# The first norm of a fused LSTM, attention and expert kernel: normalised tokens made on POOL instead of DVE

## The reference, cut to what matters

```python
x = _L0_conv_ref(x, ...)                  # 16 recurrent steps over the rows of the image
t = _to_tokens(x)                         # 16 images x 256 tokens x 96 channels
t = t + _L1_attn_ref(_ln_t(t), ...)       # 6 heads, 256 tokens read as causal windows below
t = t + _L1_ffn_ref(_ln_t(t), ...)        # 4 experts, 2 of them count, 96 -> 384 -> 96

def _ln_t(v, eps=1e-05):
    m = jnp.mean(v, axis=-1, keepdims=True)
    s = jnp.var(v, axis=-1, keepdims=True)
    return (v - m) / jnp.sqrt(s + eps)
```

## Time and profile before

| | us |
|---|---|
| median of 3 runs | 441.17 (440.37 to 441.78) |
| the profiled execution, its own time | 441.85 |
| its span, first to last instruction | 439.9 |
| PE busy in the span | 412.5 |
| DVE, ACT, POOL busy | 264.9, 252.1, 147.7 |

### The profile page before, as it was taken

The page is one execution under the profiler, slowest core; times in us unless marked ns, Lnnn a source line. Parts: engine busy times, 40 slices in busy tenths (PEclk is TensorE's granted clock), DMA queues, the critical chain, the costliest instruction groups (busy, mean ns, idle before and its releaser), DMA issues.

```text
span 439.9 us, 10654 instructions
## 1 busy us (share of the span) xinstructions
PE 412.5 (94%) x3226; PEld 346.7 (79%) x3226; DVE 264.9 (60%) x888; ACT 252.1 (57%) x701; POOL 147.7 (34%) x313
## 2 busy tenths in 40 slices
PE   4999999788899999999999999999999999999896
PEld 4999996455578878877887788788877887788686
DVE  2799998457416861785287538744863586267415
ACT  2333333356487648765865596568656764876380
POOL 6000000625513632462156305531543254236200
PEclk9999999969999999999999999999999999999999
DMA  8600000210021012101210120022002100210000
GB/s 185 168 0 0 0 0 19 63 30 17 9 60 44 3 34 53 39 1 42 52 31 0 48 55 22 0 55 52 18 0 61 46 0 7 77 24 4 7 14 18
DMA packets 16472, 14.94 MB, mean 34 GB/s; under 512 B 7586, under 2 KB 13588, under 8 KB 16452
## 3 DMA queue, kind: packets, MB, share of 16 engines
q1 hardware_dynamic: 14788, 13.87, 12.5%
q10 hardware_dynamic: 1472, 0.68, 0.6%
q0 software_dynamic: 192, 0.15, 0.1%
HBM read 3.86 MB, written 1.57 MB: 12 GB/s over the span
## 4 chain that ended last, share of the span: by engine, by line
PE 62%; DVE 16%; issue 10%; POOL 5%; ACT 2%; DVEq 1%; DMA 1%; ACTq 1%; POOLq 0%; SPq 0%
PE F L1057 13%; PE T L1015 6%; PE A L1036 6%; PE F L1073 4%; PE F L1077 4%; PE F L1074 4%; PE S L999 3%; POOL p_sb L435 3%; PE S L1001 3%; DVE fc L660 2%; DVE ig L659 2%; PE S L1004 2%; DVE t_cm L678 2%; DVE xh L713 1%; DVE nmax L735 1%
## 5 line engine op out<-in xcount | busy, mean ns | idle before, releaser
L435 POOL TENSOR_SCALAR p_sb<-p_sb,rden 128x128 f32<-128x128 f32 (+1 forms) x192 | 79.7, 431 | 121.1 <-DVE rden L741 119.0
L1057 PE MATMUL F<-w_sb,hid 128*128 128x96 f32 x768 | 97.6, 272 | 0.0
L1057 PEld LDWEIGHTS F<-w_sb,hid 128*128 128x128 f32 x768 | 95.6, 192 | 0.0
L551 ACT ACTIVATE p_sb<-S,nmax 128x128 f32<-128x128 f32 (+1 forms) x192 | 78.8, 424 | 12.7 <-DVE nmax L735 12.6
L735 DVE TENSOR_REDUCE nmax<-S 128x2 f32<-128x512 f32 (+1 forms) x80 | 50.5, 632 | 56.8 <-PE S L1004 56.7
L597 ACT ACTIVATE hid<-F,b_sb 128x512 f32<-128x512 f32 x72 | 49.5, 687 | 10.5 <-PE F L1077 9.7
L1015 PE MATMUL T<-id_sb,p_sb 128*128 128x128 f32 x288 | 48.5, 287 | 7.4 <-POOL p_sb L435 6.7
L484 ACT COPY pt_sb<-T 128x512 f32<-128x512 f32 (+1 forms) x48 | 26.4, 550 | 46.0 <-PE T L1015 46.0
L1015 PEld LDWEIGHTS T<-id_sb,p_sb 128*128 128x128 f32 x288 | 31.5, 145 | 17.6 <-POOL p_sb L435 12.2
L999 PE MATMUL S<-k_bd,q_st 96*128 96x384 f32 (+2 forms) x96 | 39.4, 417 | 3.5 <-DMA k_bd<-k_cur 2.7
L551 ACT ACTIVATION_READ_ACCUMULATOR p_sb<-S,nmax 128x1 f32 x192 | 39.7, 207 | 0.0
(11 more groups left out here) (142 smaller groups left out, 789.6 us busy)
## 6 DMA issues: line engine op xcount, KB each, us to landing
k_bd<-k_cur SPq DMA_DIRECT2D x93, 32.0 KB, 2.0
q_st<-q_cur SPq DMA_DIRECT2D x28, 96.0 KB, 2.2
k_bd<-k_cur SPq DMA_DIRECT2D x93, 16.0 KB, 1.8
t_st<-t_cm SPq DMA_DIRECT2D x7, 192.0 KB, 2.4
out_y<-y_sb SPq DMA_DIRECT2D x7, 192.0 KB, 1.9
x_pad<-in_x SPq DMA_DIRECT2D x2, 612.0 KB, 7.1
w_sb<-in_w SPq DMA_DIRECT2D x1, 576.0 KB
hid<-in_w SPq DMA_DIRECT2D x1, 576.0 KB, 6.9
```

The lines of the kernel that those rows point to most:

```text
L435: last = nc.gpsimd.tensor_scalar(p, p, rden[:, u % 3, i:i + 1], 1.0, ALU.mult, ALU.mult)
L551: last = nc.scalar.activation(p_sb[:, u % 3, i * nk:(i + 1) * nk], S[u % 2][:, i * nk:(i + 1) * nk], ACT.Exp, bias=nmax[:, u % 3, i:i + 1] ...
L1057: last = mm(dst[:, e * C:(e + 1) * C], hid[:, c, s * TT:(s + 1) * TT], w2_sb[:, c], start=False, stop=(c == NCH - 1), skip_group_check=True)
```

## The change

POOL now computes the negative means (`nm1`) as well, and makes the four `xh` itself: (token + negative mean) times inverse deviation, both numbers read for each partition. DVE keeps BN_STATS and BN_AGGR and loses `normalize1`. `rs1_step` goes up by 3 for each block.

```diff
                 nc.gpsimd.tensor_scalar(ve1[:], mv1[:, :, 1], 1e-5, None, ALU.add).then_inc(rs1_step, 1)
-                pool.wait_ge(rs1_step, 2 * n + 1)
+                nc.gpsimd.tensor_scalar(nm1[:], mv1[:, :, 0], -1.0, 1.0, ALU.mult, ALU.mult).then_inc(rs1_step, 1)
+                pool.wait_ge(rs1_step, 3 * n + 1)
                 nc.gpsimd.tensor_tensor(rs1[:], ve1[:], nhalf[:], ALU.pow).then_inc(rs1_step, 1)
+
+            def normalize1(n):
+
+                wait_alone(pool, rs1_step, 3 * n + 3)
+                for s in range(SPB):
+                    nc.gpsimd.tensor_scalar(xh[:, s], t0[:, s], nm1[:, s:s + 1], rs1[:, s:s + 1],
+                                            ALU.add, ALU.mult).then_inc(xh_done, 1)
...
                     if j == EARLY_T0 + 1 and not last:
                         rstd1(n + 1)
+                        normalize1(n + 1)
...
             rstd1(0)
+            normalize1(0)
             x1_whole(0)
...
-            def normalize1(n):
-
-                dve.wait_ge(rs1_step, 2 * n + 2)
-                for s in range(SPB):
-                    V.tensor_scalar(xh[:, s], t0[:, s], mv1[:, s, 0:1], rs1[:, s:s + 1],
-                                    ALU.subtract, ALU.mult).then_inc(xh_done, 1)
...
                     if not last:
                         if j == EARLY_T0 + 1:
                             norm1(n + 1)
-                        if j == EARLY_T0 + 2:
-                            normalize1(n + 1)
...
             norm1(0)
-            normalize1(0)
             x1_rest(0)
```

More of the change, by code:

```diff
@@ L127, in hybrid_kernel @@
         rs1 = sb("rs1", [128, SPB])
+        nm1 = sb("nm1", [128, SPB])
         xh = sb("xh", [128, SPB, C])
```

## The result

The change makes the kernel slower: 458.35 us, median of 4 runs (457.38 to 459.64), against 441.48 us of before (440.37 to 442.46). The ratio is 1.038, with a 95% interval of 1.036 to 1.040. The direction was right, the size was not: 449.8 us was forecast, and 454.0 was the upper end of the range. The profiled execution took 459.64 us with a span of 457.8, 17.9 more than before.

What follows compares the result with a forecast made beforehand. PE, working in a fixed order without slack at scale(4), was taken to bound the kernel. Six inner blocks 7.7, block 0 0.45 and ahead of the loop 0.5 us add 8.6, giving 449.8 us; range 445.8 to 454.0.

Steps and rivals of the forecast that it cites:

- No slack at scale(4), and PE can't catch up: Inner blocks, unit 4: scale(4) 1.64 us late, minus 0.36 us wait for xh, costs PE 1.28 us each, never regained.
- the 0.6 us wait for unit 8: Inner block, PE's largest remaining wait, 0.61 us for scale(8): forecast to stay unchanged; if gone, something is given back.
- The price of xh on POOL: Ahead of scale(4): four xh of 128x96 on POOL take 1.34 us, bounds 0.96 and 1.93.
- POOL's wait for itself: On POOL ahead of xh: a wait for its own earlier result, taken as 0.10 us.
- Block 0 and the part ahead of the loop: Block 0 loses 0.45 us after covered waits; the chain ahead of the loop, with nothing covering it, loses 0.5 us.
- the cover: Block 0: scale(4) had already waited from 102.19 to 102.59, so it would start only 1.34 us late.
- rival E: The clock falls as PE stands 1.6 us per block; 5 us lost in each of six blocks, near 480 us; chance 0.02.
- The sum: Whole kernel: 7.7 + 0.45 + 0.5 = 8.6 us added, giving 449.8 us.
- Rival A: PE's other waits, 0.66 us per inner block, shrink, so a block loses only 0.62 us: 445.8 us; chance 0.07.
- rival B: Four xh on POOL take 1.93 us, 0.59 more per block: 454.5 us; chance 0.08.
- Rival C: Faster: freeing PE's xh wait, 0.36 us per inner block and 0.28 in block 0, gives 438.7 us; chance 0.02.
- A rule that I weighed: At scale(4): a port shared by DVE and POOL, gain at most their overlap; trace showed none, so the sum stayed.

Runs made afterwards that it cites:

- Experiment 4: The changed kernel with POOL's four xh one step later, behind scale(4), nm staying ahead of it: 446.82 us, 1.012 of the kernel before.
- Experiment 3: The changed kernel with POOL's four xh written to a spare buffer and DVE making the real ones as before: 457.84 us, 1.038 of before.
- experiment 7: The kernel of before with 33 dummy matmuls instead of 16 ahead of block 0's first scores: 439.67 us, 0.998 of before.
- experiment 6: The kernel of before plus only the negative means (nm) on POOL, between ve and the power: 441.24 us, 1.001 of before.
- Experiment 1: The changed kernel with 11 dummy matmuls on PE ahead of its wait for scale(4), blocks 0 to 6: 450.56 us, 1.022 of before.
- experiment 11: The changed kernel with dummy matmuls ahead of scale(4), of the pre-loop transposes of xh and of the first scores: 450.83 us, 1.021 of before.
- experiment 9: The kernel of before with nm and xh slice 3 (add and multiply, own semaphore, behind scale(4)) on POOL, slices 0 to 2 on DVE: 439.90 us, 0.996.
- experiment 5: The kernel of before with xh slice 3 on POOL behind scale(4), subtracting the mean directly, slices 0 to 2 on DVE: 442.22 us, 1.004.

## Why the prediction was wrong

*No slack at scale(4), and PE can't catch up: right.* PE's new idle time is where it was foretold, POOL's p_sb ends it, the wait for xh is gone, the 0.6 us wait for unit 8 is still there (0.63 in block 2), and a block at an undisturbed clock takes 43.58 us for 43.4 foretold. Experiment 4 removes the delay of scale(4) and with it most of the cost. Experiment 3 shows that DVE's side has no part in it in the inner blocks.

*The price of xh on POOL: too low.* 1.34 us was taken for four, read off an instruction with one number per partition; they took 1.63, 0.42 each. nm cost 0.16 instead of 0.20, and POOL's wait for itself 0.20 instead of 0.10, but no handover followed ahead of scale(4), where 0.10 was counted. Together scale(4) was 1.87 us late instead of 1.64, within the bounds of 1.26 and 2.23 that the terms for xh left open. The block lost 1.42 us instead of 1.28. The six inner blocks thus cost 8.45 us for 7.7.

*Block 0 and the part ahead of the loop: too low.* They were put at 0.45 and 0.5 us, and cost 1.08 and 0.93 at an equal clock. Ahead of the loop the error is xh again (1.63 for 1.34) and the handover (0.19 for 0.10). In block 0 scale(4) was 1.88 us late at an equal clock, not 1.34. Of the difference, 0.23 are the terms above. The other 0.3 is the cover that the prediction took from the earlier trace rows, where scale(4) had waited 0.40 us for DVE's reciprocal. With the clock up there is no such wait. POOL's rows of experiment 7:

```profile
98.96 0.24 POOL L412 TENSOR_SCALAR ve<-mv 128x4 f32<-128x4 f32 x1 [0.37 <-DVE mv L707]
...
100.43 0.99 POOL L435 TENSOR_SCALAR p_sb<-p_sb,rden 128x256 f32<-128x256 f32 x2
```

How the block comes from 1.88 to 1.08 was not traced beyond this: PE's wait of 0.60 us for unit 5, counted on as cover, is gone as foretold.

*The clock: this is the step that failed.* The sum has no term for it. It was rival E, at a chance of 0.02 and left outside the range, because in the trace of before the clock had stayed at 1.00 from 110 to 122 us with 2.25 us of idle time. One execution was too weak a witness. Its longest stand in that stretch was 1.37 us, the new ones are 1.65 to 1.97; and experiment 6 showed a fall behind that very stand, 1.36 us long, in another execution. Experiment 1 fills the stand and takes 7.8 us off, some 5 in the inner blocks and 1.6 in block 0 by its profile. The price per hit was not the 5 us that E guessed: PE works for some 3.4 us at the lower level, half the clock, so 1.7 us of work are lost at most, and the block lengthens by 1.6.

*The sum.* 450.56, the changed kernel with its stand filled, is 0.8 us from the 449.8 forecast, and inside its range. Part of that closeness is luck, since the clock ahead of block 1 differs from execution to execution, and the kernel of before loses 1.3 us there itself (experiment 7). Without any fall of the clock the change costs 10.5 to 11.2 us (experiment 11) instead of 8.6; as it stands, 16.9.

*Rival A (something is given back)* didn't happen, *rival B* (xh dearer) happened to half its size. *Rival C* named the right mechanism for a gain, PE's 0.36 us at the transposes of xh, and experiment 9 collects a part of it, with one slice moved instead of four and placed behind scale(4).

*A rule that I weighed.* The port rule of the Trainium skill (SBUF — State Buffer, "Who interferes with whom") holds for a DVE instruction that uses the shared ports, and no run shows whether these do; if they did, DVE's xh would have delayed scale(4). It took 0.94 us with them and 0.93 without, so the sum was right to leave it out. The two engines do slow each other a little: 1.73 for 1.63 us on POOL in experiment 3, 1.19 for 0.96 us on DVE's three between experiments 9 and 5. The runs show no instruction of POOL that waits for a whole one of DVE.

*What stays open.* Why the stand of 1.8 us brings the clock down in some blocks and not in others. The stand is equally long in both, and the pattern differs between executions, so its length alone doesn't decide; and the fall in experiment 5 came without a stand.

## What to carry to other kernels

An engine that is busy for a third of the time can still be the one that must not be late: ask what stands behind the new work in its queue, and when the bound engine needs that. Put the new work behind it, and move only as much as the wait that it is to shorten (one slice of four won 0.4%, four slices lost 3.8%, and four slices one place later lost 1.2%, nearly half of it ahead of the loop). And where a change gives PE a new stand of nearly 2 us, price a fall of its clock as well: in each block that it hit it cost about as much as the stand itself, and one execution in which the clock stayed up elsewhere was no proof against it.

## What the runs showed of the hardware

- POOL's TENSOR_SCALAR on 128x96 with two numbers per partition takes 0.42 us as add and multiply and 0.70 us as subtract and multiply; with one number and a constant it was 0.378 us at 128 columns.
- A stand of PE (1.65 us on its matmuls, 1.81 on its weight loads), once in a block of 43 us in which it was otherwise busy, brought the granted clock from 2.4 to 1.2 GHz in three of six inner blocks, and in four of six in experiment 3, where POOL does the same work and the stand is 1.76 us on PE. PE then worked for about 3.4 us at the lower level, which lengthened the block by 1.6 us. With matmuls of no use in the stand it stayed at 1.00 in all inner blocks. Three stands of 0.28 us at the same place (experiment 4) didn't bring it down in any inner block.
- Stands of 1.36 to 1.40 us did it in some executions (experiment 6 in block 0, the changed kernel ahead of the loop) and not in others (the kernel of before, experiment 1). One fall came with no idle time of PE above 0.15 us ahead of it, behind twelve matmuls with 4 columns (experiment 5).
